# First batch's prefix sums over the first two tiles' sum, added by GpSimd, in place of both tiles; transposes of its normalised rows moved up in the queue

## Chip, cores and metric

One core of one Trainium2 chip. The metric is the device time of one execution in microseconds. A profile of one execution is read beside it; its engines are TensorE (PE, with its weight loads as PEld), VectorE (DVE), ScalarE (ACT), GpSimd (POOL) and SyncE (SP), which issues the transfers.

## What is computed

One transformer layer over x of 4 batches x 512 rows x 512 columns, in f32. Cut to what matters:

```
q, kv   = layernorm(x) @ W_q.T, layernorm(x) @ W_kv.T      # 16 heads of 32
qf, kvf = fft(q), fft(kv), each head divided by its l2 norm
kvf     = cumsum(kvf, axis=rows)                           # the prefix sums
values  = ifft(qf * kvf).real
x       = x + values @ W_o.T
x       = x + ffn(layernorm(x))      # silu(x Wg) * (x Wu), then Wd; 512 -> 1536 -> 512
```

## The kernel before

**Tiling.** A batch (b) is four tiles (t) of 128 rows. The kernel is written out engine by engine: each engine has a hand-ordered list of small steps (`tensor_program`, `scalar_program`, `vector_program`, `gpsimd_program`, `sync_program`), and a step waits on semaphores for what it needs and then runs. The order of the lists is the only order; an engine that waits holds everything behind it in its list. SP's list is the queue of nearly all transfers: a step there waits, then issues its transfers.

**Precision.** A matmul operand that must be exact to f32 is kept as two f16 parts, high (a rounded copy) and low (the rest). For the prefix sums the parts of the normalised kv rows are `ks[:, part, t]`: ScalarE writes the high part (`act_ks`, L707 to L719, the copy is L719), GpSimd the low part as a difference (`pool_ks`, L1649 to L1655).

**Prefix sums of the first batch.** `pe_tri` (L385 to L396, matmuls on L394) makes the 128x512 prefix sum of tile t: for each earlier tile s a matmul of each part with a matrix of ones (`tr16[:, 1]`), and for the tile itself a matmul of each part with the triangle (`tr16[:, 0]`). So tile 0 takes two matmuls, tile 1 four, tile 2 six, tile 3 eight. The later batches carry a row from tile to tile instead and take two matmuls each.

**What follows a tile's prefix sum.** VectorE multiplies it with q (`dve_product`, L1165 to L1185, semaphore `v_U`), GpSimd ends the complex product (`pool_product`, L1657 to L1668: a subtraction, an addition and a copy of 128x32 on L1668 that gives `p_z`), TensorE transposes the result (`pe_pT`, L398 to L406, waits for `p_z`), ScalarE and VectorE split it (`act_pT` L729, `dve_pT` L1187), and TensorE multiplies with W_o (`pe_o`, L408 to L423). `zT[:, t]` holds both parts of the transposed tile t; `act_pT(3)` and `dve_pT(3)` write `zT[:, 3]` last.

**What comes before.** VectorE sums the squares per head (`dve_sum`, L1069 to L1073, from ScalarE's squares, L682), ScalarE takes roots (`act_sqrt1`, L695), VectorE turns them into factors in four small steps (`dve_refine`, L1140 to L1148: L1142, L1144, L1146, L1148) and scales q and kv (`dve_scale`, L1159 to L1163; the kv tiles give `v_kn`). For the first batch this is done for tiles 0 and 1, then for tiles 2 and 3. Beside it W_o is folded with the inverse transform: `dve_wo_unit` (L1198 to L1204) scales the 128x128 matrix `inv`, `pe_wo_high` (L438), `act_wo_high` (L800), `pe_wo_low` (L445), `act_wo_low` (L804).

**TensorE's order around the change** (L533 to L566): kv and q of tile 2, q of tile 3, `pe_tri(0, 0)`, kv of tile 3, the four `pe_wo_high`, `pe_wo_low(0)`, `pe_tri(0, 1)`, three `pe_wo_low`, `pe_pT(0, 0)`, `pe_tri(0, 2)`, `pe_tri(0, 3)`, `pe_pT(0, 1)`, `pe_o(0, 0)`, `pe_o(0, 1)`, `pe_pT(0, 2)`, `pe_qk(1, 0, 0)`, `pe_pT(0, 3)`, `pe_o(0, 2)` and so on, then the second batch's q and kv, and the first gate of the feed-forward (`pe_first_gate`, L448 to L455). That gate reads `hT`, the transposed normalised rows after attention, high parts for its first four matmuls and low parts for the other four.

**The transposes of `hT`.** VectorE normalises (`dve_hn`), ScalarE writes the high part (`act_hT`, L739), VectorE the low part (`dve_hT`, L1239 to L1241), and SP's `sp_hT` (L1745 to L1756) issues one transposing transfer for each part. In SP's list (L1855 to L1863) loads of x for the third batch (`sp_x`) and of weights (`sp_weights`, rounded later by `act_half` and `dve_round`) stand between and before them.

Of the kernel before, what the change touches and what calls it, by code (L numbers as in the profile page):

```python
# [5 lines left out]
F32 = mybir.dt.float32  # L6
F32R = mybir.dt.float32r
# [3 lines left out]
ALU = mybir.AluOpType  # L11
ACT = mybir.ActivationFunctionType
AX = mybir.AxisListType

P = 128
# [77 lines left out]
def build(nc, x, w_q, w_kv, woT, gate_w, up_w, down_w, gs_d, us_d, ds_d, cst_d, cst2_d, id_d, out):  # L93
    ctx = ExitStack()
    with ctx:
        def sb(name, shape, dt):
            return ctx.enter_context(nc.sbuf_tensor(name, shape, dt))

        def sem(name):
            return ctx.enter_context(nc.semaphore(name))  # L100
# [10 lines left out]
        qk = sb("qk", [P, NT, 2, 512], F32)  # L111
        ks = sb("ks", [P, 2, NT, 512], F16)
        tu = sb("tu", [P, 2, 512], F32)
        pT = sb("pT", [P, 2, 512], F32R)
        h = sb("h", [P, 3, NT, 512], F32)
        hT = sb("hT", [P, 2, 2, KT, 512], F16)
        fu = sb("fu", [P, 2, 2, 512], F32R)
# [44 lines left out]
        def bank(name):  # L162
# [32 lines left out]
        d_hT = [sem("d_hT_high"), sem("d_hT_low")]  # L195
        d_zT = [sem(f"d_zT{t}") for t in range(NT)]
        a_zh, v_zl = sem("act_zh"), sem("dve_zl")
        v_most, s_bound, a_bound, v_unit2, v_gus, p_dw = (
            sem(n) for n in ("dve_most", "pe_bound", "act_bound", "dve_unit2", "dve_gus", "pool_dw"))
        d_cst, d_cst2, d_id, d_wo, d_sc, d_carry = (sem("d_" + n) for n in ("cst", "cst2", "id", "wo", "sc", "carry"))  # L200
# [73 lines left out]
            return (ba[AT["half",]] if c else bd[3])[:, 0:256]  # L274

        T_OWN = [False, True, False, True] + [True] * 12

        def pT_at(b, t):

            return zT[:, t, :, :] if b == 0 else z_parts(t)  # L280
# [102 lines left out]
            e.matmul(ba[AT["bound",]][:, 0:3], ones[:, :], bound[:, 0:3], start=True, stop=True).then_inc(s_bound, 1)  # L383

        def pe_tri(e, b, t):  # L385
            i = AT["tri", b, t]
            tiles = range(t + 1) if b == 0 else (t,)
            vacant(e, ("tri", b, t))
            e.wait_ge(p_ks, 4 * b + t + 1)
            if b == 0 and t == 0:  # L390
                e.wait_ge(a_tr, 1)
            for s in tiles:
                for part in range(2):
                    c = e.matmul(ba[i][:, :], tr16[:, 0 if s == t else 1, :], ks[:, part, s, :],  # L394
                                 start=s == tiles[0] and part == 0, stop=s == t and part == 1)
            c.then_inc(s_tri, 1)  # L396

        def pe_pT(e, b, t):  # L398
# [275 lines left out]
        def act_qk(e, b, t, w):  # L674
            n = number(b, t, w)
            i = AT["qk", b, t, w]
            e.wait_ge(s_qk, n + 1)
            if n > 1:
                e.wait_ge(v_sum, n - 1)
            if b > 0 and t == 0:  # L680
                e.wait_ge(p_z, 4 * b)
            e.activation(tu[:, n % 2, :], ba[i][:, :], ACT.Square).then_inc(a_sq, 1)  # L682
            if b > 0:
                if w == 0 and b == 1:
                    e.wait_ge(s_pT, t + 1)
                elif w == 0:
                    e.wait_ge(s_o, 4 * (b - 1) + t + 1)
                else:
                    e.wait_ge(v_hT, 4 * (b - 1) + t + 1)
            e.activation(qk[:, t, w, :], ba[i][:, :], ACT.Copy).then_inc(a_cp, 1)  # L690
# [16 lines left out]
        def act_ks(e, b, t):  # L707
            if b > 0 and t > 0:
                e.wait_ge(p_carry, 3 * (b - 1) + t)
            else:  # L710
                e.wait_ge(v_kn, 4 * b + t + 1)
            if b == 1:
                e.wait_ge(s_tri, 4)
            elif b > 1:
                e.wait_ge(s_tri, 4 * (b - 1) + t + 1)
            if b > 0:
                for part in range(2):
                    e.wait_ge(d_hT[part], 64 * b)
            e.activation(ks[:, 0, t, :], qk[:, t, 1, :], ACT.Copy).then_inc(a_ks, 1)  # L719

        def act_row(e, b, t):
# [4 lines left out]
            e.wait_ge(a_row, 3 * (b - 1) + t + 1)  # L726
            e.dma_start(qk[0:1, t, 1, :], qk[127:128, t, 1, :]).then_inc(d_carry, 16)

        def act_pT(e, t):  # L729
            e.wait_ge(s_pT, t + 1)  # L730
            e.activation(pT_at(0, t)[:, 0, :], ba[AT["pT", 0, t]][:, :], ACT.Copy).then_inc(a_pT, 1)

        def act_zh(e, b, t):
# [78 lines left out]
        def scalar_program(e):  # L812
# [38 lines left out]
            act_minus(e)  # L851
            act_qk(e, 0, 3, 0)
            act_ks(e, 0, 1)
            act_qk(e, 0, 3, 1)
            act_sqrt1(e, 0, [2, 3])
            act_wo_high(e, 0)
# [202 lines left out]
        def dve_round(e, n):  # L1059

            e.wait_ge(d_w[n], 16)
            e.tensor_scalar(part_at(near, n), stage_at(n), 2.0, -2.0, ALU.min, ALU.max, saturate=False).then_inc(v_near, 1)
            e.wait_ge(*clamped(n))
            e.wait_ge(*halved(n))
            e.scalar_tensor_tensor(out=pairs[n][1], in0=part_at(half, n), scalar=1.0, in1=part_at(near, n),
                                   op0=ALU.max, op1=ALU.mult).then_inc(v_rd, 1)
# [7 lines left out]
        def dve_stats1(e, b, t):  # L1075
            e.wait_ge(*x_landed(b, t))
            e.bn_stats(bst[:, t, :], h[:, b % 3, t, :]).then_inc(v_mv1, 1)
            e.wait_ge(v_mv1, 2 * (4 * b + t) + 1)
            e.bn_aggr(mv1[:, t, :], bst[:, t, :]).then_inc(v_mv1, 1)
# [159 lines left out]
        def dve_hT(e, b, t):  # L1239
            e.wait_ge(a_hT, 4 * b + t + 1)  # L1240
            e.tensor_tensor(ks[:, 1, t, :], qk[:, t, 1, :], ks[:, 0, t, :], ALU.subtract).then_inc(v_hT, 1)  # L1241
# [71 lines left out]
        def vector_program(e):  # L1313
# [95 lines left out]
            dve_sum(e, 1, 1, 0)  # L1409
            dve_sum(e, 1, 1, 1)  # L1410
            dve_stats1(e, 2, 0)
            dve_round(e, 4)
            dve_hT(e, 0, 3)
            dve_sum(e, 1, 2, 0)
            dve_stats1(e, 2, 1)
            dve_sum(e, 1, 2, 1)
# [232 lines left out]
        def pool_ks(e, b, t):  # L1649
# [4 lines left out]
            e.wait_ge(a_ks, 4 * b + t + 1)  # L1654
            e.tensor_tensor(ks[:, 1, t, :], qk[:, t, 1, :], ks[:, 0, t, :], ALU.subtract).then_inc(p_ks, 1)  # L1655

        def pool_product(e, b, t):  # L1657
            n = 4 * b + t
            buf = tu if T_OWN[n] else ff
            qn = qk[:, t, 0, :]  # L1660
            q_re, q_im = split_parts(qn)
            (t_re, t_im), (u_re, u_im) = split_parts(buf[:, 0, :]), split_parts(buf[:, 1, :])
            e.wait_ge(v_U, n + 1)
            e.tensor_tensor(q_re, t_re, t_im, ALU.subtract).then_inc(p_re, 1)
            e.tensor_tensor(q_im, u_re, u_im, ALU.add).then_inc(p_im, 1)
            e.wait_ge(p_re, n + 1)
            e.wait_ge(p_im, n + 1)
            e.tensor_copy(slot_0(qn), slot_0(buf[:, 0, :])).then_inc(p_z, 1)  # L1668
# [6 lines left out]
        def gpsimd_program(e):  # L1675

            pool_xl(e, 0, 1)
            pool_ones(e)
            pool_xl(e, 0, 2)
            pool_xl(e, 0, 3)  # L1680
            pool_ks(e, 0, 0)
            pool_product(e, 0, 0)
            pool_ks(e, 0, 1)
            pool_ks(e, 0, 2)
            pool_ks(e, 0, 3)
            pool_product(e, 0, 1)
            pool_xl(e, 1, 0)
            pool_product(e, 0, 2)
            pool_product(e, 0, 3)
            pool_xl(e, 1, 1)  # L1690
            pool_xl(e, 1, 2)
            pool_xl(e, 1, 3)
            pool_ks(e, 1, 0)
            pool_ks(e, 1, 1)
            pool_product(e, 1, 0)
            pool_ks(e, 1, 2)
            pool_xl(e, 2, 0)
            pool_product(e, 1, 1)
            pool_product(e, 1, 2)
            pool_ks(e, 1, 3)  # L1700
            pool_product(e, 1, 3)
            pool_xl(e, 2, 1)
            pool_xl(e, 2, 2)
            pool_xl(e, 2, 3)

            for b in range(1, NB):
                nxt = b + 1
                if b + 1 == HALF:
                    for n in range(NI // 2):
                        pool_dw(e, n)  # L1710
                pool_out(e, b - 1, 0)
                pool_out(e, b - 1, 1)
                pool_out(e, b - 1, 2)
                pool_out(e, b - 1, 3)
                if nxt < NB:
                    pool_ks(e, nxt, 0)
                    pool_product(e, nxt, 0)
                    pool_ks(e, nxt, 1)
                    pool_ks(e, nxt, 2)
                    pool_product(e, nxt, 1)  # L1720
                    pool_product(e, nxt, 2)
                    pool_ks(e, nxt, 3)
                    pool_product(e, nxt, 3)
                if b + 2 < NB:
                    pool_xl(e, b + 2, 0)
                    pool_xl(e, b + 2, 1)
                    pool_xl(e, b + 2, 2)
                    pool_xl(e, b + 2, 3)
            pool_out(e, NB - 1, 0)
            pool_out(e, NB - 1, 1)  # L1730
            pool_out(e, NB - 1, 2)
# [81 lines left out]
        def sync_program(e):  # L1813
# [39 lines left out]
            sp_xT(e, 1, 1)  # L1853
            sp_xT(e, 1, 2)
            sp_xT(e, 1, 3)  # L1855
            sp_x(e, 2, 2)
            sp_weights(e, 7)
            sp_weights(e, 8)
            sp_hT(e, 0, 0)
            sp_x(e, 2, 3)  # L1860
            sp_hT(e, 0, 1)
            sp_hT(e, 0, 2)
            sp_hT(e, 0, 3)  # L1863
            sp_weights(e, 12)
            sp_zT(e, 1, 0)
            sp_weights(e, 15)
# [112 lines left out]
```

## Time and profile before

| what | value |
|---|---|
| median of 3 runs | 419.57 us (418.23 to 420.1) |
| the profiled execution's own time | 419.01 us |
| its span in the profile | 417.2 us |
| TensorE busy | 409.6 us (98%) |
| VectorE busy | 298.0 us (71%) |
| ScalarE busy | 193.5 us (46%) |
| GpSimd busy | 109.1 us (26%) |
| TensorE's prefix-sum matmuls (L394) in the chain that ended last | 1.3% and 0.8% of the span, by bank |
| DMA, mean over the span | 80 GB/s |

The profile lists instructions with their start and duration from the span's start. The end of a matmul is modelled, so consecutive matmuls overlap in the list; the pitch between two starts is what one costs. A bracket at the end of a row gives the idle time of the engine before it and what released it. A row that ends in x12 merges twelve instructions that follow one another.

### The profile page before, as it was taken

The numbers are of one execution on the slowest core, as the hardware profiler recorded it, in microseconds if no ns is written. First come the engines' busy times: TensorE is split into PE (matmuls) and PEld (weight loads), VectorE is DVE, ScalarE is ACT, GpSimd is POOL, SyncE is SP. The second block draws the span as 40 slices with busy tenths as digits, with TensorE's granted clock in tenths as the row PEclk, the third lists the DMA queues.
The fourth block names the chain that finished last, engine by engine and source line by source line (L and its number), as shares of the span: only waits on it lengthen the run. The fifth ranks groups of instructions, "written<-read, shape, count | busy, mean of one in ns | idle before, by whom it ended". The sixth has DMA issues, their size and how long they took to land.

```text
span 417.2 us, 5555 instructions
## 1 busy us (share of the span) xinstructions
PE 409.6 (98%) x1921; PEld 205.5 (49%) x1921; DVE 298.0 (71%) x516; ACT 193.5 (46%) x324; POOL 109.1 (26%) x114
## 2 busy tenths in 40 slices
PE   8999999999999999999999999999999999999995
PEld 4744454445555554454555555454444444445442
DVE  5998998999989699997984972167855853422235
ACT  3687756587736245445242563345543341132220
POOL 0133551015154137043541013032462001300003
PEclk9999999999999999999999999999999999999999
DMA  8996546800181153232112015411112041200002
GB/s 256 259 267 240 166 113 160 169 0 2 38 241 52 26 77 68 59 123 78 28 26 50 2 25 102 75 38 64 26 26 52 0 70 32 101 2 0 2 0 101
DMA packets 57691, 33.55 MB, mean 80 GB/s; under 512 B 49472, under 2 KB 50112, under 8 KB 57536
## 3 DMA queue, kind: packets, MB, share of 16 engines
q1 hardware_dynamic: 57232, 32.93, 31.0%
q8 instruction: 15, 0.25, 0.3%
q10 hardware_dynamic: 432, 0.28, 0.2%
q14 instruction: 12, 0.10, 0.1%
HBM read 17.44 MB, written 4.19 MB: 52 GB/s over the span
## 4 chain that ended last, share of the span: by engine, by line
PE 91%; DVE 3%; ACT 2%; DMA 1%; POOL 1%; issue 1%; SPq 1%; DVEq 0%
PE bu L476 19%; PE bg L476 19%; PE bd L503 19%; PE ba L376 14%; PE ba L421 8%; PE bd L376 3%; PE bd L344 2%; DMA h<-x_dram 1%; PE ba L394 1%; PE bd L421 1%; PE bd L394 1%; PE bd L362 1%; PE bu L421 1%; POOL xs L1642 1%; PE bd L498 0%
## 5 line engine op out<-in xcount | busy, mean ns | idle before, releaser
L476 PE MATMUL bu<-hT,gu 128*128 128x512 f16 x384 | 90.7, 379 | 0.0
L476 PE MATMUL bg<-hT,gu 128*128 128x512 f16 x376 | 89.0, 379 | 0.1
L1257 DVE SCALAR_TENSOR_TENSOR ff<-bu,us,sl 128x512 f32<-128x512 f32 x47 | 35.1, 748 | 53.9 <-PE bu L476 50.7
L756 ACT ACTIVATE sl<-bg,gs 128x512 f32<-128x512 f32 x48 | 33.0, 687 | 78.1 <-PE bg L476 77.1
L376 PE MATMUL ba<-wf,xT 128*128 128x512 f16 x288 | 63.2, 379 | 0.0
L476 PEld LDWEIGHTS bu<-hT,gu 128*128 128x128 f16 x384 | 37.5, 98 | 45.5 <-DVE ff L1257 0.6
L476 PEld LDWEIGHTS bg<-hT,gu 128*128 128x128 f16 x376 | 35.6, 98 | 43.4 <-issue 3.9
L503 PE MATMUL bd<-dw,fu 128*128 128x512 f32 x192 | 51.1, 411 | 0.0
L1673 POOL TENSOR_TENSOR h<-ff,h 128x512 f32<-128x512 f32 x14 | 17.5, 1269 | 121.3 <-DVE ff L1299 121.3
L376 PEld LDWEIGHTS ba<-wf,xT 128*128 128x128 f16 x288 | 27.8, 98 | 34.2 <-issue 1.1
L1642 POOL TENSOR_TENSOR xs<-xn,xs 128x512 f16<-128x512 f32 x15 | 20.4, 1368 | 79.3 <-ACT xs L668 79.3
L503 PEld LDWEIGHTS bd<-dw,fu 128*128 128x128 f32 x192 | 36.0, 188 | 9.6 <-DVE fu L1264 0.4
L503 PE MATMUL bd<-own,half 128*128 128x512 f16 x162 | 38.6, 379 | 0.0
L1655 POOL TENSOR_TENSOR ks<-qk,ks 128x512 f16<-128x512 f32 x16 | 21.0, 1315 | 48.9 <-ACT ks L719 48.9
L421 PE MATMUL ba<-wo,qk 128*128 128x512 f16 x144 | 32.6, 379 | 0.0
L1073 DVE TENSOR_REDUCE S<-tu 128x16 f32<-128x512 f32 x32 | 21.5, 676 | 11.2 <-ACT tu L682 11.2
L1264 DVE TENSOR_TENSOR half<-ff,half 128x512 f16<-128x512 f32 x23 | 19.3, 838 | 11.9 <-ACT half L762 11.7
L503 PEld LDWEIGHTS bd<-own,half 128*128 128x128 f16 x162 | 15.8, 98 | 19.0 <-DVE half L1264 0.4
L682 ACT ACTIVATE tu<-ba 128x512 f32<-128x512 f32 x24 | 14.3, 595 | 22.2 <-PE ba L376 22.1
L1162 DVE TENSOR_TENSOR qk<-qk,sc 128x512 f32<-128x512 f32 x32 | 23.1, 738 | 0.2
L1264 DVE TENSOR_TENSOR fu<-ff,fu 128x512 fp32r<-128x512 f32 x24 | 20.8, 872 | 3.2 <-ACT fu L762 3.0
L762 ACT ACTIVATE half<-ff 128x512 f16<-128x512 f32 x23 | 14.3, 623 | 18.4 <-PE ba L498 7.5
(210 smaller groups left out, 540.7 us busy)
## 6 DMA issues: line engine op xcount, KB each, us to landing
h<-x_dram SPq DMA_DIRECT2D x16, 256.0 KB, 4.1
out_dram<-h SPq DMA_DIRECT2D x14, 256.0 KB, 2.0
hT<-w_q_dram SPq DMA_DIRECT2D x4, 256.0 KB, 4.1
gu<-w_kv_dram SPq DMA_DIRECT2D x4, 256.0 KB, 4.1
hT<-gate_w_dram SPq DMA_DIRECT2D x2, 512.0 KB, 3.7
hT<-up_w_dram SPq DMA_DIRECT2D x2, 512.0 KB, 6.0
gu<-woT_dram SPq DMA_DIRECT2D x1, 1024.0 KB, 5.3
hT<-down_w_dram SPq DMA_DIRECT2D x2, 512.0 KB, 5.0
```

Source lines behind the costliest of these rows:

```text
L376: m = e.matmul(ba[i][:, :], xT[:, b % 2, part_x, k, P * t:P * t + P], wf[:, w, part_w, k, :], start=k == 0 and part_x == part_w, stop=k == ...
L421: m = e.matmul(ba[i][:, :], src[:, part_p, P * j:P * j + P], wo[:, part_w, j, :], start=j == 0 and part_p == part_w, stop=j == KT - 1 and ...
L476: m = e.matmul(bk[:, :], gu[:, c, 4 * w + k, col:col + P], hT[:, b % 2, part, k, :], start=k == 0 and part == 0, stop=k == KT - 1 and part ...
L503: m = e.matmul(bd[t][:, :], fu_at(n)[:, part, P * t:P * t + P], (dw if n < HALF * NI else dw16)[:, i, :], start=i == 0 and part == 0, stop ...
L756: e.activation(sl[:, n % 2, :], bg[:, :], ACT.Silu, scale=gs[:, i:i + 1]).then_inc(a_silu, 1)
L1073: e.tensor_reduce(S[:, t, NH * w:NH * w + NH], v, AX.X, ALU.add).then_inc(v_sum, 1)
L1162: e.tensor_tensor(split_heads(qk[:, t, w, :]), split_heads(qk[:, t, w, :]), head_scale(t, w), ALU.mult).then_inc(v_kn if w else v_qn, 1)
L1257: e.scalar_tensor_tensor(out=ff[:, n % 2, :], in0=bu[:, :], scalar=(us if b < HALF else us2)[:, i:i + 1], in1=sl[:, n % 2, :], op0=ALU.mul ...
L1264: e.tensor_tensor(fu_at(n)[:, 1, :], ff[:, n % 2, :], high.bitcast(F32) if n < HALF * NI else high, ALU.subtract).then_inc(v_fu, 1)
L1642: e.tensor_tensor(xs[:, t % 2, 1, :], xn[:, t % 2, :], xs[:, t % 2, 0, :], ALU.subtract).then_inc(p_xl, 1)
L1655: e.tensor_tensor(ks[:, 1, t, :], qk[:, t, 1, :], ks[:, 0, t, :], ALU.subtract).then_inc(p_ks, 1)
L1673: e.tensor_tensor(hh, y_at(b, t), hh, ALU.add).then_inc(p_out, 1)
```

## The change

The first batch's prefix sums of tiles 2 and 3 read one summed tile, `sum_parts`, in place of tiles 0 and 1. GpSimd adds the two normalised tiles in f32 (`pool_sum`), ScalarE rounds the sum to f16 (`act_sum`), GpSimd takes the difference (`pool_sum_low`). The two parts lie in `zT[:, 3]`, which is free until tile 3 is transposed; `act_pT(3)` waits for the last prefix sum. In `pe_tri` the matmuls over whole earlier tiles now stand ahead of the wait for the tile's own low part. The tile `pT`, which nothing used, makes room for `sums`. In VectorE's list `dve_hT(0, 3)` changes places with `dve_round(4)`, and in SP's list the transposes of `hT` move ahead of loads.

```diff
-        pT = sb("pT", [P, 2, 512], F32R)
+        sums = sb("sums", [P, 512], F32)
...
+        sum_parts = zT[:, 3, :, :]
...
         def pe_tri(e, b, t):
             i = AT["tri", b, t]
-            tiles = range(t + 1) if b == 0 else (t,)
+            whole = [] if b > 0 or t == 0 else [ks[:, :, 0, :]] if t == 1 else [sum_parts] + [ks[:, :, s, :] for s in range(2, t)]
             vacant(e, ("tri", b, t))
-            e.wait_ge(p_ks, 4 * b + t + 1)
             if b == 0 and t == 0:
                 e.wait_ge(a_tr, 1)
-            for s in tiles:
+            if b == 0 and t == 2:
+                e.wait_ge(a_sum, 1)
+                e.wait_ge(p_sumlo, 1)
+            for n, parts in enumerate(whole):
                 for part in range(2):
-                    c = e.matmul(ba[i][:, :], tr16[:, 0 if s == t else 1, :], ks[:, part, s, :],
-                                 start=s == tiles[0] and part == 0, stop=s == t and part == 1)
+                    e.matmul(ba[i][:, :], tr16[:, 1, :], parts[:, part, :], start=n == 0 and part == 0, stop=False)
+            e.wait_ge(p_ks, 4 * b + t + 1)
+            for part in range(2):
+                c = e.matmul(ba[i][:, :], tr16[:, 0, :], ks[:, part, t, :],
+                             start=not whole and part == 0, stop=part == 1)
             c.then_inc(s_tri, 1)
...
+        def act_sum(e):
+            e.wait_ge(p_sum, 1)
+            e.activation(sum_parts[:, 0, :], sums[:, :], ACT.Copy).then_inc(a_sum, 1)
+
         def act_pT(e, t):
             e.wait_ge(s_pT, t + 1)
+            if t == 3:
+                e.wait_ge(s_tri, 4)
...
             act_ks(e, 0, 1)
+            act_sum(e)
             act_qk(e, 0, 3, 1)
...
+            dve_hT(e, 0, 3)
             dve_round(e, 4)
-            dve_hT(e, 0, 3)
...
+        def pool_sum(e):
+            e.wait_ge(v_kn, 2)
+            e.tensor_tensor(sums[:, :], qk[:, 0, 1, :], qk[:, 1, 1, :], ALU.add).then_inc(p_sum, 1)
+
+        def pool_sum_low(e):
+            e.wait_ge(a_sum, 1)
+            e.tensor_tensor(sum_parts[:, 1, :], sums[:, :], sum_parts[:, 0, :], ALU.subtract).then_inc(p_sumlo, 1)
...
             pool_ks(e, 0, 0)
+            pool_sum(e)
             pool_product(e, 0, 0)
             pool_ks(e, 0, 1)
+            pool_sum_low(e)
             pool_ks(e, 0, 2)
...
             sp_xT(e, 1, 3)
+            sp_hT(e, 0, 0)
+            sp_weights(e, 7)
+            sp_hT(e, 0, 1)
             sp_x(e, 2, 2)
-            sp_weights(e, 7)
-            sp_weights(e, 8)
-            sp_hT(e, 0, 0)
-            sp_x(e, 2, 3)
-            sp_hT(e, 0, 1)
             sp_hT(e, 0, 2)
             sp_hT(e, 0, 3)
+            sp_weights(e, 8)
+            sp_x(e, 2, 3)
             sp_weights(e, 12)
```

## Rows read from the trace of the kernel before

**Rows 1.** The page: busy time of TensorE (busy us, share, instructions) and granted clock by slices.
```profile
PE 409.6 (98%) x1921; PEld 205.5 (49%) x1921; DVE 298.0 (71%) x516; ACT 193.5 (46%) x324; POOL 109.1 (26%) x114
...
PEclk9999999999999999999999999999999999999999
```
**Rows 2.** Timeline of TensorE, 40 to 58 us (start us, duration us, what, count).
```profile
42.84 1.03 PE L394 MATMUL bg<-ks,tr 128*128 128x512 f16 x4
43.70 0.59 PE L445 MATMUL bd<-wo,minus 128*128 128x512 f16 x2
44.78 0.39 PE L445 MATMUL ba<-wo,minus 128*128 128x512 f16 x1 [0.48 <-ACT wo L800]
...
45.61 3.18 PE L394 MATMUL bd<-ks,tr 128*128 128x512 f16 x14
48.83 0.63 PE L405 MATMUL bd<-cst,qk 128*128 128x128 f32 x4
```
**Rows 3.** Timeline of GpSimd, 34 to 50 us.
```profile
38.54 0.73 POOL L1664 TENSOR_TENSOR qk<-ff 128x256 f32<-128x256 f32 x1 [3.02 <-DVE ff L1185]
...
40.10 0.24 POOL L1668 COPY qk<-ff 128x32 f32<-128x32 f32 x1
40.29 1.15 POOL L1655 TENSOR_TENSOR ks<-qk,ks 128x512 f16<-128x512 f32 x1
44.31 2.27 POOL L1655 TENSOR_TENSOR ks<-qk,ks 128x512 f16<-128x512 f32 x2 [2.87 <-ACT ks L719]
...
48.09 0.59 POOL L1668 COPY qk<-tu 128x32 f32<-128x32 f32 x1
```
**Rows 4.** Timeline of ScalarE, 36 to 46 us.
```profile
39.39 0.60 ACT L682 ACTIVATE tu<-bu 128x512 f32<-128x512 f32 x1 [1.42 <-PE bu L376]
...
43.60 0.63 ACT L719 ACTIVATE ks<-qk 128x512 f16<-128x512 f32 x1 [0.57 <-DVE qk L1162]
```
**Rows 5.** Timeline of VectorE, 35 to 49 us.
```profile
35.53 0.69 DVE L1162 TENSOR_TENSOR qk<-qk,sc 128x512 f32<-128x512 f32 x1
...
36.33 0.29 DVE L1204 TENSOR_SCALAR sl<-sl,size 128x128 f32<-128x128 f32 x1
...
38.38 0.68 DVE L1073 TENSOR_REDUCE S<-tu 128x16 f32<-128x512 f32 x1
39.71 0.69 DVE L1077 BATCH_NORM_STATS2 bst<-h 128x6 f32<-128x512 f32 x1 [0.65 <-DMA h<-x_dram]
...
42.10 0.22 DVE L1144 SCALAR_TENSOR_TENSOR Q<-y 128x64 f32<-128x64 f32 x1
42.36 0.23 DVE L1146 TENSOR_TENSOR Q<-Q,S 128x64 f32<-128x64 f32 x1
...
42.88 1.29 DVE L1162 TENSOR_TENSOR qk<-qk,sc 128x512 f32<-128x512 f32 x2
```
**Rows 6.** Timeline of all engines, 205.5 to 208.5 us: VectorE beside GpSimd.
```profile
205.74 1.16 POOL L1655 TENSOR_TENSOR ks<-qk,ks 128x512 f16<-128x512 f32 x1 [1.16 <-ACT ks L719]
205.84 1.07 DVE L1123 TENSOR_TENSOR bound<-bound 128x1 f32<-128x1 f32 x1
...
206.95 0.15 DVE L1125 TENSOR_SCALAR bound<-bound 128x1 f32<-128x1 f32 x1
...
207.52 0.78 DVE L1132 TENSOR_SCALAR us<-us,bound 128x12 f32<-128x12 f32 x1
207.54 0.73 POOL L1665 TENSOR_TENSOR qk<-tu 128x256 f32<-128x256 f32 x1
```
**Rows 7.** The hT transposes: SP's issues, their landing, the first gate, the next statistics.
```profile
72.30 7.76 SPq L1756 DMA_TRANSPOSE hT<-ks  x6
...
hT<-ks SPq DMA_TRANSPOSE x2, 2.5
...
81.25 1.89 PE L453 MATMUL bg<-hT,gu 128*128 128x512 f16 x8
...
84.54 0.69 DVE L1077 BATCH_NORM_STATS2 bst<-h 128x6 f32<-128x512 f32 x1
```

More of the change, by code:

```diff
@@ L197, in build @@
         a_zh, v_zl = sem("act_zh"), sem("dve_zl")
+        p_sum, a_sum, p_sumlo = sem("pool_sum"), sem("act_sum"), sem("pool_sumlo")
         v_most, s_bound, a_bound, v_unit2, v_gus, p_dw = (
```

## The prediction

> **What bounds the kernel now.** I read the page first. TensorE is busy 409.6 us, 98% of the span, and its granted clock is full in all 40 slices [rows 1]. So a matmul that goes away is worth its time only if TensorE does not wait for something else just behind it. The second view is therefore TensorE's timeline around the prefix sums [rows 2]. Four matmuls of L394 start at 42.84 and the next group starts at 43.70, which is 0.86 us for four: 0.216 us each, back to back. The fourteen matmuls of tiles 2 and 3 start at 45.61. At the same pitch they let the next instruction start at 45.61 + 14 x 0.216 = 48.63. The transposes behind them (`pe_pT(0, 1)`) start at 48.83. The page shows no wait there, because the modelled end of the last matmul covers it, but 0.2 us are missing.
>
> The third view, GpSimd's timeline, says what those 0.2 us are [rows 3]. `pe_pT(0, 1)` needs `p_z` of tile 1, the last instruction of `pool_product(0, 1)`: the copy at 48.09 that ends at 48.68. GpSimd runs from 44.31 to there almost without a pause: two `pool_ks` (2.27 us), the two halves of the product, the copy. What let it start at 44.31 was ScalarE's `act_ks(0, 2)`, 43.60 to 44.23 [rows 4], which waited for VectorE's scaling at 42.88, which stands behind the four small steps of `dve_refine` (42.10 and 42.36 are the second and third). These wait for the sum over tile 3's kv squares, which stands behind the statistics at 39.71, and these for a load of x [rows 5]. That chain contains no matmul of the prefix sums. It, not TensorE, decides when `pe_pT(0, 1)` starts, and from there TensorE runs on almost gapless.
>
> **The change, part by part.** *Removed:* tile 1 of the first batch keeps four matmuls, tile 2 goes from six to four, tile 3 from eight to six. Four matmuls less at 0.216 us are 0.86 us, with their weight loads. All four lie between 45.61 and 48.63, ahead of the wait for `p_z`. If nothing else moves, TensorE is through with tile 3 at 47.77 and stands 1.06 us instead of 0.2 us. Gain at the end: 0. The new order inside `pe_tri` (whole tiles first, then the wait for the own tile) only shifts work within the same cover. `pe_pT(0, 1)` is not moved ahead.
>
> *Added on ScalarE:* `act_sum`, a 128x512 copy to f16, by the row of `act_ks` 0.63 us. It stands behind `act_ks(0, 1)` and ahead of the square that waits 1.42 us for TensorE until 39.39 [rows 4], so it costs nothing as long as the sum is there by about 38.8. Behind it stand the two roots that the chain needs, so a late sum would cost one for one.
>
> *Added on GpSimd:* a sum and a subtraction over 128x512. The nearest rows take 1.15 us [rows 3]. `pool_sum` waits for the second `v_kn`, which VectorE gives at 35.53 + 0.69 = 36.22 [rows 5]; GpSimd starts some 0.08 us after a release (44.31 behind 44.23), so it runs 36.30 to 37.45, before the product at 38.54. `pool_sum_low` follows `pool_ks(0, 1)`, from 41.42 to 42.57, ahead of 44.31, where GpSimd stood idle for 2.87 us. On GpSimd's own queue both are free; if that cover were gone each would cost 1.15 us.
>
> *What they do to VectorE* is the real term. [Rows 6] show one-element operations beside GpSimd. With two SBUF inputs one took 1.07 us (L1123, from 205.84) and ended with GpSimd's instruction at 206.90; its like with one input took 0.15 us at 206.95, beside the next one. A 12-element tensor_scalar from 207.52 took 0.78 us and also ended with GpSimd's, which had started 0.02 us later. So GpSimd's instruction in progress holds such a VectorE instruction to its end, and the held one then ends about as late as its own time less 0.13 us. The Trainium skill (GPSIMD Engine Reference, 1. Specifications) says the same in general: contention with VectorE instructions in a 2-port mode or with two SBUF inputs. It speaks against this change. The note in Advanced Engine Details and Errata, Mode Summary, names 2-port instructions alone; by it the 1.07 us would not be there, so the trace sides with the wider wording.
>
> First meeting: `dve_wo_unit` scales 128x128 in SBUF at 36.33, a tensor_scalar, 0.29 us [rows 5]. `pool_sum` starts 0.03 us ahead of it and holds it until 37.45 + 0.16 = 37.61 instead of 36.62: VectorE is 0.99 us late. That runs on through its queue to the sum at 38.38, whose successor could have started at 38.98 but waited for the load until 39.71. The slack of 0.73 us takes most of it; 0.26 us are left in the chain. GpSimd's product and `pool_ks(0, 1)` move by 0.99 us too, so `pool_sum_low` runs from 42.4 to 43.6.
>
> Second meeting: the steps of `dve_refine` at 42.10 and 42.36, now 0.26 us later, both have two SBUF inputs. The first fits in at the end of `pool_ks(0, 1)`, the second is held to about 43.75 instead of 42.59. The chain is then 1.2 us late, and with it `act_ks(0, 2)`, GpSimd, the last `wo` piece on TensorE (44.78) and `pe_pT(0, 1)`. Bounds for this term: 0 from below (the small steps pass between two instructions), 0.99 + 1.15 = 2.1 us from above (two full holds, no slack). I take 1.2, since [rows 6] give the nearest cases and both end with GpSimd's instruction.
>
> *Moved:* the transposes of `hT` for the first batch go ahead of `sp_weights(8)` and `sp_x(2, 3)`, partly of `sp_x(2, 2)` and `sp_weights(7)`; `dve_hT(0, 3)` goes ahead of `dve_round(4)`. Before, SP issued the last six of the eight without a pause from 72.30 to 80.06; the last two landed 2.5 us after their issue, so about 81.3. TensorE's first gate matmul starts at 81.25, and its low half, which needs the last one, four matmuls later at 82.1 [rows 7]. There is no gap: worth 0 today, and a cover of 0.8 us more if TensorE came earlier. Two loads of x and two of weights now stand behind some or all of the transposes. The first work on any of them is the statistics of x(2, 2) at 84.54 [rows 7]; its load goes out after four of the eight transposes, and even one issued only at 80.06 would have 4.5 us. `dve_round(4)` comes 0.6 us later (a subtraction) and its weights are used from the third gate on. I take 0. Without the move, a full gain of 0.86 us would just meet this landing and lose about 0.1 us.
>
> **The sum.** The profiled execution took 419.01 us, 1.8 us of it around the span. 419.01 - 0 + 1.2 = 420.2 us. Its time lies 0.56 us under the median of the three runs (419.57), whose spread of 1.9 us is larger than any term here. A measurement of this kernel tells about 0.5% (2.1 us) from no change, so the forecast is no change that can be told, on the slow side.
>
> **The rivals.**
> *One hold only, 0.4.* If VectorE's tensor_scalar at 36.33 gets in first (the margin is 0.03 us), `pool_sum` waits instead, `pool_sum_low` runs 41.42 to 42.57, and only the step at 42.10 is held, to 42.66 instead of 42.32: +0.34, so 419.4. If two-input instructions were not held at all, the first meeting's 0.26 us alone would remain: 419.3. For it: the narrow margin. Against it: at 207.52 VectorE was even 0.02 us ahead and lost.
> *Nothing but the wait, 0.* The four matmuls leave, TensorE waits for `p_z` as computed, no hold lands on the chain: 419.0. Against it: [rows 6].
> *The full gain.* 419.01 - 0.86 = 418.2. It needs `p_z` of tile 1 to come 1 us earlier, or the 0.2 us of [rows 2] to be no wait. In its favour is only that part of the copy's 0.59 us is itself a hold (the copy at 40.10 takes 0.24), which could give 0.35.
> *Slower.* TensorE would stand twice within 4 us: 0.48 + 1.2 = 1.7 us before 44.78's matmul and 1.06 us before `pe_pT(0, 1)`. If the granted clock fell to its lower level over the group behind that (twelve matmuls of 2.59 us, which would take twice that at 1.2 GHz), it would cost 2.6 us more: 422.8. It decides from a granted clock below 1.0 in the stretch 50 to 55. Against it: [rows 1] show full clock in all slices, the pause of 0.48 us included.
>
> **How the numbers follow.** Forecast 1.2 us late: 0.45. One hold: 0.21. Only the wait: 0.16. Gain, full or in part: 0.12. Slower by the clock or a double hold: 0.06. The forecast is the likeliest case. The range goes from the full gain (418.2) to the upper bound of the holds less what the chances leave out, 421.6, which also takes in the spread of the runs on either side. Faster by over 0.5% would need 2.1 us, and no case gives more than 0.86: 0.02, for the noise. Slower: the last rival and a part of the upper bound, 0.06. Within 0.5%: 0.92.
>
> **What would show it.** L394 with 16 instead of 20 matmuls in the first batch; the start of `pe_pT(0, 1)` counted from the span's start: near 50.0 by the forecast, 49.2 with one hold, 48.8 with none, 48.0 with the gain. `dve_wo_unit`'s tensor_scalar near 1.3 us instead of 0.29, and one step of `dve_refine` above 1 us. A step there at 0.22 us would make the forecast wrong; so would a `p_z` of tile 1 that comes earlier than 48.6.

## The result and the profile after

The changed kernel took 420.06 us (median of 22 runs) beside 419.44 us for the kernel before (22 runs): ratio 1.0024, 95% interval 1.0014 to 1.0033, so it is 1.0 us slower by the ratio on record (0.6 to 1.4). The two medians alone differ by 0.62 us, the means of the runs by 0.89 us. The forecast was 420.2 us and no change that can be told at 0.5%. In its profiled execution the span is 418.6 us, 1.4 us above the 417.2 of before.

The page of the changed kernel, its span and busy times:

```profile
span 418.6 us, 5549 instructions
...
PE 408.0 (97%) x1917; PEld 204.9 (49%) x1917; DVE 299.9 (72%) x516; ACT 194.0 (46%) x325; POOL 110.5 (26%) x116
```

TensorE has four matmuls less and is busy 1.6 us less than in [rows 1], and yet the span is longer. What it waited for is in the waits of TensorE in the changed kernel (us in total, times, longest):

```profile
PE ba L454 <- ACT wo L815: 1.6, 1, 1.6
...
PE bd L414 <- POOL qk L1692: 1.1, 1, 1.1
PE bg L485 <- ACT sl L771: 1.0, 1, 1.0
```

The first is the last `wo` piece, 0.48 us before [rows 2]. The second is `pe_pT(0, 1)`, which waits for `p_z`. The third, 1.0 us near 101 us, was not in the prediction.

TensorE's timeline of the changed kernel, its first prefix sum and the second tile's transposes:

```profile
35.55 0.59 PE L403 MATMUL ba<-ks,tr 128*128 128x512 f16 x2
...
45.29 0.39 PE L454 MATMUL ba<-wo,minus 128*128 128x512 f16 x1 [1.61 <-ACT wo L815]
...
47.68 0.59 PE L403 MATMUL bd<-ks,tr 128*128 128x512 f16 x2
49.34 0.63 PE L414 MATMUL bd<-cst,qk 128*128 128x128 f32 x4 [1.07 <-POOL qk L1692]
```

The first tile's prefix sum starts 0.61 us earlier than in the kernel before (35.55 instead of 36.16). Nothing of the change acts before that point, and over the profiles of this study it lies anywhere from 35.16 to 36.47. So positions are compared from there: `pe_pT(0, 1)` starts 13.79 us behind it, and 12.67 us in the kernel before (48.83 - 36.16), so 1.12 us late. The forecast was 1.2 us (50.0 - 36.16 = 13.84 us). Counted from the span's start, as the prediction wanted it, the transposes stand at 49.34, which its list would read as one hold (49.2). That reading is wrong here, because the whole stretch began 0.61 us sooner. The run with the operations alone, which begins as the kernel before does (36.17), has them at 49.96.

Why is seen on VectorE, with GpSimd beside it, in the changed kernel (rows of both engines' timelines, VectorE first):

```profile
35.72 1.32 DVE L1220 TENSOR_SCALAR sl<-sl,size 128x128 f32<-128x128 f32 x1
...
40.22 0.65 DVE L1089 TENSOR_REDUCE S<-tu 128x16 f32<-128x512 f32 x1
...
41.78 0.22 DVE L1160 SCALAR_TENSOR_TENSOR Q<-y 128x64 f32<-128x64 f32 x1
42.04 1.06 DVE L1162 TENSOR_TENSOR Q<-Q,S 128x64 f32<-128x64 f32 x1
```

```profile
35.69 1.27 POOL L1675 TENSOR_TENSOR sums<-qk 128x512 f32<-128x512 f32 x1 [0.78 <-DVE qk L1178]
...
40.71 1.16 POOL L1671 TENSOR_TENSOR ks<-qk,ks 128x512 f16<-128x512 f32 x1
41.83 1.19 POOL L1679 TENSOR_TENSOR zT<-sums,zT 128x512 f16<-128x512 f32 x1
```

`pool_sum` starts 0.03 us ahead of the scaling of `inv`, which takes 1.32 us instead of 0.29 and ends 0.08 us behind GpSimd's operation (37.04 and 36.96). Then `pool_ks(0, 1)` ends at 41.87, and the first two-input step of `dve_refine` passes in 0.22 us. `pool_sum_low` starts at 41.83, and the next step takes 1.06 us instead of the 0.23 of [rows 5].

The third wait stands in the second batch's carry: ScalarE issues a copy of one row (2 KB) from partition 127 to partition 0, GpSimd adds it, ScalarE copies to f16, and behind that copy stands the gate activation that TensorE needs. The kernel before (rows of the timeline of all engines):

```profile
93.16 0.61 ACTq L727 DMA_DIRECT2D qk<-qk  x1
...
96.47 1.25 POOL L1653 TENSOR_TENSOR qk<-qk 1x512 f32<-1x512 f32 x1 [5.72 <-DMA qk<-qk]
...
97.76 0.63 ACT L719 ACTIVATE ks<-qk 128x512 f16<-128x512 f32 x1 [2.83 <-POOL qk L1653]
...
98.94 0.69 ACT L756 ACTIVATE sl<-bg,gs 128x512 f32<-128x512 f32 x1
```

And the changed kernel:

```profile
93.72 0.61 ACTq L736 DMA_DIRECT2D qk<-qk  x1
...
97.73 1.42 POOL L1669 TENSOR_TENSOR qk<-qk 1x512 f32<-1x512 f32 x1 [6.43 <-DMA qk<-qk]
...
99.19 0.63 ACT L728 ACTIVATE ks<-qk 128x512 f16<-128x512 f32 x1 [3.70 <-POOL qk L1669]
...
100.37 0.69 ACT L771 ACTIVATE sl<-bg,gs 128x512 f32<-128x512 f32 x1
...
101.20 1.02 PE L485 MATMUL bg<-hT,gu 128*128 128x512 f16 x4 [1.00 <-ACT sl L771]
```

From the issue to GpSimd's addition it is 4.01 us instead of 3.31. Put together for this pair of profiles: -0.61 (earlier start, not the change's) + 1.12 (holds) + 0.92 (from the first gate to the fifth, 19.44 us instead of 18.52) = 1.43 us, against 1.4 between the two spans; the stretch between, from `pe_pT(0, 1)` to the first gate, is 32.42 us in both. Two of the three terms are not the holds, and they nearly cancel; whether the last one is in the medians too is a question for the experiments.

### The profile page after: what moved, and what is told of

The parts are those of the page before. It is cut to its first block, busy times and chain, and to the rows that moved or that the text cites. A ratio compares the mean times of both kernels' runs of the same rounds, so it can differ in the third digit from the quotient of the medians.

```text
span 418.6 us, 5549 instructions
## 1 busy us (share of the span) xinstructions
PE 408.0 (97%) x1917; PEld 204.9 (49%) x1917; DVE 299.9 (72%) x516; ACT 194.0 (46%) x325; POOL 110.5 (26%) x116
## 4 chain that ended last, share of the span: by engine, by line
PE 85%; DVE 5%; issue 3%; DMA 2%; POOL 2%; ACT 1%; SPq 0%; ACTq 0%; POOLq 0%; DVEq 0%
PE bu L485 19%; PE bg L485 19%; PE bd L512 18%; PE ba L379 14%; PE ba L430 8%; PE ba L403 1%; DMA gu<-woT_dram 1%; PE bd L347 1%; PE bd L430 1%; PE bd L379 1%; DMA qk<-qk 1%; POOL ks L1671 1%; DVE qk L1178 1%; PE bu L430 1%; DVE S L1089 1%
```

## The experiments

Theory: the removed matmuls lie ahead of a wait and are worth nothing, and the whole price is that GpSimd's two new operations hold VectorE. Rivals: the removal is worth 0.86 us and something larger hides it; the moved transposes and loads cost the time; and, after the result, the copy of the carry. All ratios are against the kernel before on the same chip.

**Operations without the removal.** `pool_sum`, `act_sum`, `pool_sum_low` as in the change, the lists and the matmuls of before:

```diff
         def pe_tri(e, b, t):
+            if b == 0 and t == 2:
+                e.wait_ge(a_sum, 1)
+                e.wait_ge(p_sumlo, 1)
             for s in tiles:
```

> The three added operations (pool_sum, act_sum, pool_sum_low) with the old twenty matmuls in pe_tri and the old lists of VectorE and SP; the sum is made and not read. Hold theory: everything the change costs comes from these three, so the time is that of the changed kernel, about 1.0 us over the kernel before; one step of dve_refine takes about 1.06 us, and TensorE's pause before pe_pT(0, 1) shrinks to 0.2 us. Rival (the new order of pe_tri or of the lists costs the time): no more than 0.2 us over the kernel before.

420.29 us, ratio 1.0024 (1.0013 to 1.0036), as the changed kernel. Rows of its timelines, VectorE and TensorE:

```profile
42.65 1.06 DVE L1160 TENSOR_TENSOR Q<-Q,S 128x64 f32<-128x64 f32 x1
```

```profile
46.70 3.18 PE L401 MATMUL bd<-ks,tr 128*128 128x512 f16 x14
49.96 0.63 PE L412 MATMUL bd<-cst,qk 128*128 128x128 f32 x4
```

The transposes start 13.79 us behind the first prefix sum (36.17), to the hundredth as in the changed kernel, with all twenty matmuls. The removal is worth nothing there. The span is that of the changed kernel too, but not term by term. There is no early start and no wait in the carry, and 0.38 us are lost between the transposes and the first gate, of which 0.22 are a wait for a transfer of `xT` at 56.43.

**The removal alone.** Tiles 2 and 3 leave tile 0 out, nothing is added:

```diff
-            tiles = range(t + 1) if b == 0 else (t,)
+            tiles = range(t > 1, t + 1) if b == 0 else (t,)
```

> The kernel before without the four matmuls on tile 0 in the sums of tiles 2 and 3, which leaves tile 0's rows out of those sums; nothing is added. Theory that pe_pT(0, 1) waits for p_z: 0 us against the kernel before, with a pause of about 1.06 us on TensorE ahead of those transposes at 48.8. Rival (the removal is worth its time): 0.86 us faster, no pause over 0.3 us.

418.98 us, ratio 0.9991 (0.9976 to 1.0006): no gain that can be told; the full 0.86 us (0.9980) lies inside the interval, so the time alone doesn't exclude it. TensorE's timeline does:

```profile
44.77 2.57 PE L394 MATMUL bd<-ks,tr 128*128 128x512 f16 x10
47.98 0.63 PE L405 MATMUL bd<-cst,qk 128*128 128x128 f32 x4 [0.64 <-POOL qk L1668]
```

After ten matmuls instead of fourteen it stands and waits for GpSimd. The next matmul could have started at 44.77 + 10 x 0.216 = 46.93; it starts 1.05 us later. The transposes stand 12.42 us behind the first prefix sum, 0.25 us sooner than before, because in this run the load that the statistics wait for was earlier (38.87 - 35.56 = 3.31 us instead of 3.55).

**Lists as before.** The changed kernel with VectorE's and SP's lists of before:

```diff
-            dve_hT(e, 0, 3)
             dve_round(e, 4)
+            dve_hT(e, 0, 3)
```

(and SP's list likewise.)

> The changed kernel with VectorE's and SP's lists of before (dve_hT(0, 3) behind dve_round(4), the hT transposes behind the loads). Hold theory: as the changed kernel, 1.0 us over the kernel before, no wait at the first gate. Rival (the moved loads cost time at the carry of the second batch, where the changed kernel's profile shows TensorE waiting 1.0 us for ScalarE): back to within 0.2 us of the kernel before.

420.39 us, ratio 1.0026 (1.0014 to 1.0039). `pe_pT(0, 1)` stands at 13.78 us, and there is no wait at the first gate without the move. The rival, that the moved loads cost the time, is out.

**Lists alone.** The kernel before with only the two lists changed.

> The kernel before with only the lists of VectorE and SP changed as the change has them. Prediction's step: 0 us against the kernel before, hT's last transposes landed about 1 us earlier, nothing waits for the loads that moved back. Rival: the wait of 1.0 us for ScalarE at the second batch's carry, seen in the changed kernel's profile, comes with these lists: 0.5 to 1.0 us slower.

418.78 us, ratio 0.9996 (0.998 to 1.0011). No worth of the moves can be told either way, and the wait of the rival isn't there. Rows of SP's and TensorE's timelines:

```profile
74.41 5.21 SPq L1756 DMA_TRANSPOSE hT<-ks  x4
```

```profile
80.99 1.89 PE L453 MATMUL bg<-hT,gu 128*128 128x512 f16 x8
```

The last transposes are issued by 79.62 instead of 80.06 [rows 7]. Counted from the first prefix sum that is 43.83 us instead of 43.90, so the move brought them 0.07 us and not the expected 1 us. The gate starts as soon as TensorE is there, in this run as before.

**No hold.** The changed kernel, GpSimd's order changed:

```diff
             e.wait_ge(v_kn, 2)
+            e.wait_ge(v_inv, 2)
...
             pool_sum(e)
+            pool_sum_low(e)
+            pool_ks(e, 0, 1)
             pool_product(e, 0, 0)
-            pool_ks(e, 0, 1)
-            pool_sum_low(e)
```

> The changed kernel, but pool_sum also waits until VectorE has scaled inv (v_inv 2), and GpSimd's list has pool_sum_low and pool_ks(0, 1) ahead of pool_product(0, 0), so that GpSimd should be idle while dve_refine runs. Hold theory: both holds go, the tensor_scalar takes 0.29 us and each step of dve_refine 0.23 us, and the time is that of the kernel before (0 within 0.2 us), with a pause of 1.06 us before pe_pT(0, 1). Rival (the cost lies elsewhere): still 0.8 us or more over it.

419.73 us, ratio 1.0001 (0.9987 to 1.0016). VectorE's and TensorE's rows:

```profile
36.30 0.29 DVE L1220 TENSOR_SCALAR sl<-sl,size 128x128 f32<-128x128 f32 x1
...
41.85 0.64 DVE L1162 TENSOR_TENSOR Q<-Q,S 128x64 f32<-128x64 f32 x1
```

```profile
48.73 0.63 PE L414 MATMUL bd<-cst,qk 128*128 128x128 f32 x4 [1.07 <-POOL qk L1693]
```

The first hold is gone; of the second 0.41 us stay, now from half of the product. The transposes start at 12.59 us, where the kernel before has 12.67. That this is no later has a second reason: the load of x was there sooner, so the sum behind the statistics stands 3.85 us after the first prefix sum instead of 4.38, which gives back about 0.5 us at the steps of `dve_refine`. With TensorE's pause of 1.07 us unchanged, the cost went with the holds, within an interval of -0.5 to +0.7 us.

**One hold each.** First only `e.wait_ge(v_inv, 2)` in `pool_sum` (first hold gone), then only GpSimd's new order (second hold gone).

> The changed kernel, but pool_sum also waits until VectorE has scaled inv; GpSimd's order stays. Hold theory: the tensor_scalar takes 0.29 us again, pool_sum_low still runs at about 41.4 to 42.6 and holds one step of dve_refine for 0.3 to 0.4 us: 0.3 to 0.4 us over the kernel before. Rival (each hold costs its own full length): the second still costs about 1 us.

419.21 us, ratio 1.0 (0.9985 to 1.0014). Rows of VectorE and GpSimd:

```profile
41.72 1.02 DVE L1160 SCALAR_TENSOR_TENSOR Q<-y 128x64 f32<-128x64 f32 x1
```

```profile
41.50 1.16 POOL L1680 TENSOR_TENSOR zT<-sums,zT 128x512 f16<-128x512 f32 x1
```

The hold is 0.8 us, not 0.34: the load of x came sooner, so the step met GpSimd's operation near its start. The sooner load gives back 0.5 us, and `pe_pT(0, 1)` stands at 12.97 us, 0.30 late. In time, the forecast of 0.3 to 0.4 us and none can't be told apart.

> The changed kernel, but GpSimd's list has pool_sum_low and pool_ks(0, 1) ahead of pool_product(0, 0); pool_sum still starts beside VectorE's scaling of inv. Hold theory: the tensor_scalar takes 1.32 us, which the wait for the load of x hides up to about 0.3 us, and at most half of the halves of the product (0.7 us) meets dve_refine: 0.3 to 0.6 us over the kernel before. Rival (the first hold is what costs): 1.0 us over it, as the changed kernel.

419.64 us, ratio 1.0009 (0.9995 to 1.0022), the scaling of `inv` takes 1.32 us, the steps of `dve_refine` 0.28 and 0.23 us, `pe_pT(0, 1)` at 12.99 us, 0.32 late: what the wait for the load doesn't hide of the first hold. The times of these two can't be told from 0.3 us or from each other; the positions can. The two together cost 1.12 us, which is 0.80 for the second hold and 0.32 for the first; the 0.30 of the run before is 0.80 less what its sooner load gave back.

**The pause filled.** The kernel without holds, with `pe_o(0, 0)` split in two:

```diff
-            pe_pT(e, 0, 1)
-            pe_o(e, 0, 0)
+            pe_o(e, 0, 0, range(2))
+            pe_pT(e, 0, 1)
+            pe_o(e, 0, 0, range(2, KT))
```

> The kernel without holds of the last call, and half of pe_o(0, 0), six matmuls of 0.216 us, moved into TensorE's pause of 1.07 us before pe_pT(0, 1). Theory that the gain was only unused: pe_pT(0, 1) starts 0.2 to 0.3 us later, pe_o(0, 1) then waits for dve_pT(1) and starts about 0.4 us earlier than in the kernel without holds, and the time is 0.3 to 0.4 us under the kernel before. Rival (VectorE's list sets the next starts too, or the carry of the second batch does): 0 us.

419.29 us, ratio 0.9998 (0.9986 to 1.001). TensorE's rows:

```profile
48.26 1.46 PE L430 MATMUL bd<-wo,zT 128*128 128x512 f16 x6
...
51.96 2.75 PE L430 MATMUL ba<-wo,zT 128*128 128x512 f16 x12 [0.52 <-DVE zT L1208]
```

As expected, `pe_o(0, 1)` now waits for VectorE, which sets the next starts too. It stands 15.56 us behind the first prefix sum (36.40), 0.16 us sooner than in the kernel before and 0.08 sooner than without the filling (51.78 - 36.14 = 15.64), not the expected 0.4; and the carry's wait of 1.00 us is there again. The rival of this expectation, 0 us, is what came.

**The carry's copy.** The wait near 101 us was in the profiles of the changed kernel, the removal alone, no hold, second hold gone and pause filled (1.0 us each) and, at 0.3 to 0.4, in two more; it was absent in the three with twenty matmuls.
```profile
GB/s 0 0 0 0 0 0 0 0 0 137 8 9 0 0 0 0 0 1 0 0 0 0 0 0 0 0 0 0 0 0 0 0 0 0 0 0 0 0 0 0
...
q8 instruction: 1, 0.02, 1.2%
...
qk<-qk ACTq DMA_DIRECT2D x1, 2.0 KB, 3.2
```

The changed kernel:

```profile
GB/s 0 0 0 0 0 0 0 0 0 0 8 9 0 0 0 137 0 0 0 0 0 0 0 1 0 0 0 0 0 0 0 0 0 0 0 0 0 0 0 0
...
q8 instruction: 1, 0.02, 1.2%
...
qk<-qk ACTq DMA_DIRECT2D x1, 2.0 KB, 3.9
```

The lone 1 behind the gap is the end of the row. Thirty of its 32 packets have moved by 1.4 us after the issue, in every profile. The last two follow at 2.06 us in the kernel before and at 2.84 in the changed kernel, and that is where the 16 KB packet ends, by its start and its length (1.16 + 0.92 = 2.08 and 1.89 + 0.96 = 2.85). So the row seems to wait for this packet's end, wherever it starts in those profiles, and it lands 1.0 to 1.1 us behind.

With four matmuls and their weight loads less, the packet starts 0.7 us later against the row in this pair. Over all profiles the rule is looser: it starts 1.0 to 1.2 us after the row's issue in the three kernels with twenty matmuls, and 1.1 to 1.9 us after it in the seven with sixteen. The removal alone has it at 1.07 and still lands its row late, at 3.5 us, since there the packet takes 1.34 us. Tiny matmuls (8 columns) in the warm-up put the place back:

```diff
             pe_warm(e, 14)
+            for n in range(4):
+                e.matmul(bd[3][:, 0:8], ks[:, 0, 0, 0:P], ks[:, 0, 0, 0:8], start=True, stop=True)
```

> The changed kernel with four extra matmuls of 8 columns behind the first warm-up ones, so that TensorE's list is as long again as before up to the second batch. Theory of a second wait (the four missing matmuls and weight loads shift TensorE's 16 KB instruction fetch by eight instructions, onto the one-row copy of the second batch's carry, which then lands after 3.4 to 3.9 us instead of 3.1): the fetch starts 0.1 to 0.2 us ahead of the copy's packets again, the copy lands after 3.1 us, TensorE's wait of 1.0 us for ScalarE near 101 us goes, and the time is 0.3 to 0.9 us under the changed kernel. Rival (the landing varies by itself): the copy takes 3.4 us or more here too and the time is the changed kernel's.

420.04 us, ratio 1.0022 (1.0009 to 1.0036): in time not to be told from the changed kernel. The 16 KB are back ahead of the row (slice 8), the row lands after 3.3 us, the wait near 101 us is 0.27 instead of 1.00 us. The expectation was half right in the profile, where the wait is shorter and not gone, and wrong in time, where its 0.3 to 0.9 us did not come.

> As the kernel with four tiny matmuls, with thirty-two: the fetch should come about 6 us ahead of the carry's copy. Theory of the fetch: the copy lands after 3.1 us or less, no wait near 101 us. Rival: 3.4 us or more. The extra 28 tiny matmuls stand in the warm-up, where up to 1 us of them is not hidden by anything I can name, so the time may be up to 1 us over the one with four.

The row's transfers with thirty-two:

```profile
GB/s 0 0 0 0 0 0 0 0 0 0 8 10 0 0 0 0 0 0 0 0 0 0 0 0 0 0 0 0 0 0 0 0 0 0 0 0 0 0 0 0
...
qk<-qk ACTq DMA_DIRECT2D x1, 2.0 KB, 1.7
```

Without the 16 KB in its way (the packet starts 1.3 us ahead of the row's issue and ends 0.4 us ahead of it) all 32 packets have moved by 1.4 us, the same row lands after 1.7 us, and there is no wait near 101 us. The whole takes 421.88 us, ratio 1.0067 (1.0046 to 1.0088), 1.8 us over the kernel with four, where at most 1 us was expected. The profile has 1.6 us of it behind the fifth gate. One new wait of 0.8 us is seen there, for a transpose of `zT` before `pe_o` at 151.18. What delays it, and where the rest is, stays open.

> The kernel without holds and with the four tiny matmuls. If the two causes add up (hold and fetch): no wait near 101 us, one of 1.06 us before pe_pT(0, 1), and the time is that of the kernel before, 0 within 0.2 us, or slightly under. If only the hold matters: the same as the kernel without holds.

419.38 us, ratio 1.0004 (0.9988 to 1.0019), row landed after 3.1 us, no wait near 101 us, `pe_pT(0, 1)` at 12.84 us. One two-input step was still held here, by half of the product (0.77 us instead of 0.22). In time it is as the theory of both causes has it, and within what the other allows.

> The kernel with the filled pause and the four tiny matmuls, the candidate to beat both kernels: 0.2 to 0.5 us under the kernel before if the carry lands in time; 0 if it doesn't, since all gained before the carry is then lost in its wait.

418.93 us, ratio 0.999 (0.9976 to 1.0003), no wait near 101 us. It is the best of the changed forms, but it can't be told from the kernel before; the load of x was 1.2 us late for the statistics in its profile, so the filled pause gave nothing there.

**What the times say together.** With both holds the ratio is 1.0022 to 1.0026 (the changed kernel, the operations without the removal, the lists as before, the four tiny matmuls). Without them, or with half of the second left, it is 0.9990 to 1.0004 (no hold, the pause filled, each with and without tiny matmuls, the removal alone, the lists alone), and with one hold 1.0000 and 1.0009. The copy of the carry leaves no such mark. Three pairs of kernels differ only in the four tiny matmuls, which took 0.7 to 1.0 us of wait away from each profile, and their ratios are 1.0024 and 1.0022, 1.0001 and 1.0004, 0.9998 and 0.9990. On average the four matmuls gain 0.1 us, an estimate, since each interval is some 0.4 to 0.6 us to either side.

The positions of the profiles, in us: the start of the first prefix sum, then counted from it the statistics that need the load of x and `pe_pT(0, 1)`, then from there to the first gate, from the first gate to the fifth, and the landing of the row. From the fifth gate to the end it is 317.3 to 317.5 us in all of them but the one with thirty-two tiny matmuls (319.1).

| kernel | first prefix sum | to statistics | to `pe_pT(0, 1)` | from it to gate 1 | gate 1 to 5 | row lands |
|---|---|---|---|---|---|---|
| before | 36.16 | 3.55 | 12.67 | 32.42 | 18.52 | 3.2 |
| changed | 35.55 | 3.86 | 13.79 | 32.42 | 19.44 | 3.9 |
| operations without removal | 36.17 | 3.85 | 13.79 | 32.80 | 18.48 | 3.1 |
| removal alone | 35.56 | 3.31 | 12.42 | 32.42 | 19.38 | 3.5 |
| lists as before | 36.47 | 3.85 | 13.78 | 32.41 | 18.73 | 3.4 |
| lists alone | 35.79 | 3.67 | 12.78 | 32.42 | 18.52 | 3.1 |
| no hold | 36.14 | 2.94 | 12.59 | 32.41 | 19.45 | 3.7 |
| first hold gone | 36.26 | 3.06 | 12.97 | 32.92 | 18.79 | 3.4 |
| second hold gone | 35.56 | 3.84 | 12.99 | 32.42 | 19.44 | 3.8 |
| pause filled | 36.40 | 3.49 | 13.15 | 31.84 | 19.45 | 3.6 |
| changed, four tiny | 35.77 | 3.86 | 13.82 | 32.42 | 18.70 | 3.3 |
| changed, thirty-two tiny | 36.06 | 3.86 | 13.80 | 32.42 | 18.27 | 1.7 |
| no hold, four tiny | 35.16 | 3.18 | 12.84 | 32.42 | 18.47 | 3.1 |
| filled, four tiny | 36.38 | 4.08 | 13.52 | 31.83 | 18.39 | 3.0 |

In the two filled kernels `pe_pT(0, 1)` comes behind half of `pe_o(0, 0)`, so their third and fourth numbers are not to be set beside the others. Where the first hold is (3.84 to 3.86), VectorE and not the load sets the start of the statistics. In the rest the load does, and it moves the transposes by up to about 0.5 us from run to run.

## Why the prediction was right, point by point

- **The removal is worth 0.** Right: the same position of `pe_pT(0, 1)` with sixteen and with twenty matmuls (13.79 us), and a pause of about 1.06 us that is simply longer by what was removed.
- **The first hold.** Forecast 1.28 us for the scaling of `inv`, of which 0.26 reach the chain. Measured 1.32 us; the sum behind it stands 4.67 us after the first prefix sum instead of 4.38: 0.29. Two small errors cancel in the 1.28: `pool_sum` took 1.27 us and not the 1.15 of its nearest row, and the held scaling ended 0.08 us behind it, not 0.16.
- **The second hold.** Forecast: the first step passes, the second is held, 1.2 us late in all. Measured: just so, 1.06 us for L1162 and 1.12 us in all. By the prediction's own rule the step would end at about 43.7 and not 43.75, 1.1 us late; the difference is below what matters here.
- **One hold only.** The mechanism was right and its size was not: the hold at the step of 42.10 was put at 0.34 us and measured 0.80 us with the first hold gone, since the load of x, which sets when the step comes, differs by some tenths from run to run.
- **The moved lists are worth 0.** Right as far as can be told: 0.9996 (0.998 to 1.0011). That the transposes would have cost the full gain 0.1 us could not be tried, since no form had that gain.
- **The Trainium skill's two wordings** (GPSIMD Engine Reference, 1. Specifications, and the narrower one in Advanced Engine Details and Errata, Mode Summary). L1162 has two SBUF inputs and 64 elements, and it was held 0.83 us: the wider wording holds here too.
- **The rival of the clock.** TensorE stood 1.61 and 1.07 us within about 4 us, and the granted clock was 1.00 from 50 to 55 us; the twelve matmuls behind the pause took the 2.59 us (49.80 to 52.39) that they take in the kernel before.
- **Not foreseen: the carry.** 0.92 us of the changed kernel's profile come from it, and the sum of the prediction has no term for it. The times show no such cost: the operations without the removal have the holds and no such wait and take as long (420.29 us) as the changed kernel (420.06), and so do the four tiny matmuls (420.04). How often the row lands late over many executions stays open, since only the profiled execution of each kernel shows it.
- **How far the total is luck.** The term is not: 1.12 us of holds were measured in position, and 1.0 us (0.6 to 1.4) in time. That 420.2 lies so near to 420.06 is in part. The sum started from one execution of 419.01 us, 0.4 us under the median of 22 runs, and added a term that is 0.1 to 0.2 us large. And that the two profiles differ by 1.4 us, near the forecast 1.2, rests on an early start and a late row that nearly cancel.
- **The range.** Its upper end, 421.6, does not follow from the terms given: 419.01 and the upper bound of 2.1 us are 421.1. Nothing measured hangs on it.

## What to carry to other kernels

Before work is taken off the busiest engine, look at the instruction behind it: if that one waits, even for 0.2 us that a modelled matmul end hides, what is removed ahead of it becomes pause. When an operation goes to GpSimd, list the VectorE instructions with two SBUF inputs, or tensor_scalar from SBUF to SBUF, that will run beside it; each can be held to the end of GpSimd's instruction, and a small one no less (1.06 us for 64 elements a partition, 1.07 for one). Of tensor_scalar the rows have both: those of 128 and of 12 elements a partition were held, that of one element was not [rows 6]. Compare profiles from a common instruction near the change, not from the start of the span, and let the terms of a pair of profiles be checked by the times of several kernels before they are called a cost.
